# A four-layer decoder on one core: first keys ahead of the statistics, weight splits moved, and cross attention's quantised inputs behind the squares

## The chip, the core and the metric

The kernel is one program on one core of a Trainium2 chip. Its engines are TensorE (PE for its matmuls, PEld for its weight loads), VectorE (DVE), ScalarE (ACT), GpSimd (POOL) and SyncE (SP), which issues the DMAs. The metric is the device time of one execution in microseconds. Three runs of the kernel before took 2043.24 to 2045.09 us, with a median of 2044.54 us.

## What is computed

The reference is a decoder of four layers over x of shape (8, 128, 256), each layer with an attention, a cross attention and a feed-forward part, and each part added to x behind a layer norm. Three parts that follow each other matter here: the experts of layer 1, and the attention and the cross attention of layer 2. Cut to their core:

```python
# layer 1: one shared and seven routed experts (L1f in the kernel)
output = silu(x @ Ws1) * (x @ Wsg) @ Ws2
for e in range(7):
    output = output + _expert_ffn(x, W1[e], Wg[e], W2[e]) * w_e[..., None]
# layer 2, attention (L2a): 16 heads of 16, causal, with a slope per head
attn = softmax(q @ k.T / 4 + alibi + causal); y = attn @ v; out = y @ W_o
# layer 2, cross attention (L2x): 16 query heads, 8 key groups, head size 128
def _div_clamp_fp8(x, scale):
    y = jnp.clip(x.astype(jnp.float32) / scale, -FP8_MAX, FP8_MAX)
    y = y.astype(jnp.bfloat16).astype(jnp.float32)
    return _fp8_roundtrip(y)
q = _ln(linear(_div_clamp_fp8(ln_out, q_in_scale), wq)); k = ...; v = ...
core = _gqa(q, k, v)                 # self part
xout = _gqa(qx, kx, vx)              # part over the context
catq = _div_clamp_fp8(concatenate([core, xout]), proj_smooth)
out = catq @ wproj.T * scales
```

`_div_clamp_fp8` is what the kernel calls quantising: it divides by a scale, clips, and rounds to the grid of an 8-bit float.

## The kernel before, in words

All five engines run hand-ordered instruction lists and meet at counting semaphores. The order on an engine is the order of the Python calls that issue its instructions; nothing is scheduled by a planner. The eight rows of 128 positions of x are called tiles.

**The experts (L1f).** 16 steps s, each one expert on half of the tokens. PE computes the gate and up products (L4025, L4033), ACT the silu (L1808), DVE their product (`L1f_prod`, L2898), PE the down product (L4050), and DVE adds it, weighted, to x (`L1f_add`, L2908, four instructions of 128x256). Beside that, the weights of the next layer are split in three bf16 parts each, high, middle and low: ACT copies the high part (`L2x_hi`, L1833, or `L2q_hi`), a subtraction leaves the rest (`L2x_rest`, L2934 on DVE), ACT copies the middle part (`L2x_mid`, L1838), and a second subtraction gives the low one (`L2x_lo`, L2940 on DVE). p0 to p7 are the pieces of the output projection's weights, q0 to q3 and qx0 to qx3 those of the two query projections. The raw pieces p0 to p7 come by DMA through two buffers, so p7 is loaded (L1034 on SP) only when p6's low part is done.

**The attention (L2a).** One tile per step i. For the first tile PE computes queries and keys (`L2a_qk`, L4107), ACT copies them (`L2a_qTc`, L1904), DVE spreads the keys with a mask (`L2a_keys`, L3030), PE computes the values (`L2a_value`, L4113) and the scores (`L2a_scores`, L4122), DVE adds the bias (`L2a_bias`, L3036) and takes the maximum (L3042), POOL subtracts it (`L2a_sub`, L1320), ACT takes the exponential (L1916), PE transposes (L4130) and multiplies by the values (L4142, L4146), DVE divides (L3046, L3050), and PE projects (L4152). Ahead of it DVE makes the mask (L3057), fills constants (L3058 to L3062) and takes the statistics of tiles 2 to 7 (`L2a_stats`, L3021, L3024), from which ACT computes the factors (L1892, L1894) for POOL's norm (`L2a_norm`, L1316). The splits of p7 and qx0 to qx2 run in these steps, one instruction of ACT and one of POOL in each.

**The cross attention (L2x).** 64 steps i, eight for each tile: four groups of heads in the self part, four in the part over the context. In a step PE projects q, k, v (`L2x_project`, L4223 and L4227 to L4237), ACT squares q and k (L1992, L1994), DVE sums the squares (`L2x_ss`, L3121), ACT computes the factor (L2004, L2008), DVE scales q and k (`L2x_norm`, L3127, L3128), and PE transposes them (`L2x_qkTr`, L4243, L4247), which ends PE's step. The steps overlap: in step i DVE also takes the maximum of the scores of step i-1 (`L2x_max`, L3132), smooths the output of step i-2 (`L2x_smooth`, L3143) and takes step i-1's reciprocal (L3138); ahead of them stands `L2x_magic` for step i-3 (L3149, L3151, L3153), the first half of the quantising of the attention's output, whose second half is POOL's `L2x_cat` (L1356, L1358). POOL also multiplies the probabilities (`L2x_prob`, L1350). In steps i with i % 8 in (4, 5, 6, 7) and i < 56, 28 of the 64, DVE quantises one of the four inputs of the next tile (`L2x_quantise`, L3009, L3013, L3015, L3017), and POOL finishes it (`L2x_quantise_sum`, L1343, L1346).

## Time and profile before

| | |
|---|---|
| median of three runs | 2044.54 us (2043.24 to 2045.09) |
| the profiled execution | 2038.3 us, of which the span is 2036.6 us |
| busy: PE, DVE, ACT, POOL | 1780.2, 1495.5, 1100.1, 1118.3 us (87%, 73%, 54%, 55% of the span) |
| mean granted clock of TensorE | 0.946 |
| first keys of the attention (L3030) | start at 708.35 us |
| first sum of squares of the cross attention (L3121) | starts at 807.50 us |
| last sum of squares of the cross attention | starts at 1291.51 us |

A time in a row is counted from the start of the span. "L12" is line 12 of the kernel before. A row of the timeline gives start, duration, engine, line and operation, and in square brackets how long the engine stood idle before it and what released it. The granted clock is 1.00 at full speed and 0.50 at half.

### The profile page before, as it was taken

Reading aid. Unit: us, or ns where it says so; the run is one execution under the profiler, and the core shown is the slowest. Engines: PE = TensorE matmul, PEld = TensorE weight load, DVE = VectorE, ACT = ScalarE, POOL = GpSimd, SP = SyncE. Lnnn points to the kernel's source line nnn. Section 1 sums busy time; section 2 is a strip of 40 time slices with the busy share of each in tenths; the row PEclk is TensorE's granted clock in tenths of the full one; section 3 lists DMA queues with packets and bytes.
Section 4 is the critical chain, followed back from the end, with each engine's and each line's share of the span. In section 5 each row is a group of like instructions: output and inputs, shape, how many; then the busy total and the mean of one; then the engine's idle time right before and its main releaser. Section 6 shows DMA issues by size and latency. Waiting matters only on the chain.

```text
span 2036.6 us, 30008 instructions
## 1 busy us (share of the span) xinstructions
PE 1780.2 (87%) x10774; PEld 1291.2 (63%) x10822; DVE 1495.5 (73%) x2379; ACT 1100.1 (54%) x2325; POOL 1118.3 (55%) x823
## 2 busy tenths in 40 slices
PE   6777779799999987999999999878888888998998
PEld 5111148555565575777777778767777765667887
DVE  5788952557546675888898888689999877866654
ACT  4444431334423354666666666567677556754443
POOL 4699950212496074555555555599999952223321
PEclk9788889779999998999999999989999979998999
DMA  4211001140110100000000001200000002000000
GB/s 158 61 37 37 0 1 42 39 186 6 67 79 26 42 12 1 1 1 1 1 1 1 1 1 54 74 0 1 1 1 1 27 1 87 1 1 1 6 9 9
DMA packets 21099, 54.89 MB, mean 27 GB/s; under 512 B 8783, under 2 KB 12536, under 8 KB 18648
## 3 DMA queue, kind: packets, MB, share of 16 engines
q1 hardware_dynamic: 20952, 52.97, 7.9%
q8 instruction: 87, 1.43, 0.3%
q14 instruction: 60, 0.49, 0.1%
HBM read 44.57 MB, written 1.05 MB: 22 GB/s over the span
## 4 chain that ended last, share of the span: by engine, by line
PE 57%; DVE 23%; ACT 8%; issue 7%; POOL 4%; DMA 0%; POOLq 0%; DVEq 0%; ACTq 0%
DVE sbuf L2463 3%; PE psum L4388 3%; PE psum L4050 2%; PE psum L4033 2%; PE psum L4223 2%; PE psum L4025 2%; PE psum L3678 2%; PE psum L4286 2%; DVE sbuf L3015 2%; DVE sbuf L3013 2%; PE psum L4255 2%; ACT sbuf L2116 2%; PE psum L4681 1%; PE psum L4235 1%; DVE sbuf L3151 1%
## 5 line engine op out<-in xcount | busy, mean ns | idle before, releaser
L1397 POOL TENSOR_TENSOR sbuf<-sbuf 128x1035 f32<-128x1035 f32 x128 | 245.0, 1943 | 0.9 <-ACT sbuf L2084 0.9
L4388 PE MATMUL psum<-sbuf 128*128 128x128 f32 (+1 forms) x1024 | 146.4, 294 | 56.3 <-ACT sbuf L2116 41.5
L2116 ACT ACTIVATE sbuf<-sbuf 128x1001 f32<-128x1001 f32 (+1 forms) x128 | 142.0, 1142 | 83.0 <-DVE sbuf L3278 58.9
L4388 PEld LDWEIGHTS psum<-sbuf 128*128 128x128 f32 (+1 forms) x1024 | 128.2, 154 | 76.4 <-ACT sbuf L2116 55.1
L1155 POOL TENSOR_TENSOR sbuf<-sbuf 128x1024 f32<-128x1024 f32 x64 | 149.8, 2355 | 16.5 <-DVE sbuf L2463 16.5
L1350 POOL TENSOR_TENSOR sbuf<-sbuf 128x512 f32<-128x512 f32 x64 | 72.8, 1137 | 153.8 <-DVE sbuf L3138 153.8
L2463 DVE TENSOR_TENSOR_SCAN sbuf<-psum,sbuf 128x1024 f32<-128x1024 f32 x64 | 144.6, 2278 | 12.5 <-POOL sbuf L1155 7.6
L3270 DVE SCALAR_TENSOR_TENSOR psum<-sbuf,psum 128x1024 f32<-128x1024 f32 (+1 forms) x96 | 122.3, 1274 | 21.6 <-PE psum L4378 15.1
L3624 PE MATMUL psum<-sbuf 96*128 96x512 bf16 x256 | 81.2, 426 | 60.5 <-DVE sbuf L2463 34.5
L1543 ACT ACTIVATE psum<-psum,sbuf 128x1016 f32<-128x1016 f32 x64 | 68.7, 1081 | 119.0 <-PE psum L3624 119.0
L3278 DVE TENSOR_TENSOR sbuf<-psum,sbuf 128x1024 f32<-128x1024 f32 (+1 forms) x96 | 116.4, 1213 | 3.3
L1356 POOL TENSOR_TENSOR sbuf<-sbuf 128x512 f32<-128x512 bf16 x64 | 77.5, 1212 | 52.7 <-DVE sbuf L3153 51.0
L3624 PEld LDWEIGHTS psum<-sbuf 96*128 96x128 bf16 x256 | 18.4, 101 | 137.1 <-DVE sbuf L2463 67.9
L2024 ACT ACTIVATE sbuf<-psum,sbuf 128x128 f32<-128x128 f32 x256 | 90.4, 365 | 23.5 <-DVE sbuf L3132 21.8
L4223 PE MATMUL psum<-sbuf 128*128 128x512 bf16 x336 | 90.1, 386 | 6.3 <-issue 3.9
L4286 PE MATMUL psum<-sbuf 128*128 128x256 bf16 x768 | 94.3, 273 | 0.9 <-POOL sbuf L1358 0.9
L1471 POOL TENSOR_TENSOR sbuf<-sbuf 128x1024 f32<-128x1024 f32 x16 | 30.7, 1921 | 116.7 <-DVE sbuf L3474 116.6
L3121 DVE TENSOR_REDUCE sbuf<-sbuf 128x6 f32<-128x768 f32 x64 | 60.8, 950 | 40.6 <-ACT sbuf L1994 40.6
L4286 PEld LDWEIGHTS psum<-sbuf 128*128 128x128 bf16 x768 | 74.9, 98 | 17.6 <-POOL sbuf L1358 1.7
L1358 POOL TENSOR_TENSOR sbuf<-sbuf 128x512 bf16<-128x512 f32 x64 | 81.5, 1274 | 5.0
L3657 PE MATMUL psum<-sbuf 128*32 128x512 f32 x256 | 77.7, 738 | 4.3 <-POOL sbuf L1155 4.3
L1405 POOL TENSOR_TENSOR sbuf<-sbuf 128x1024 f32<-128x1024 f32 (+1 forms) x32 | 68.7, 2146 | 19.7 <-DVE sbuf L3270 19.7
(695 smaller groups left out, 4995.3 us busy)
## 6 DMA issues: line engine op xcount, KB each, us to landing
sbuf<-sbuf SPq DMA_DIRECT2D x50, 128.0 KB, 2.4
sbuf<-w_gu_d SPq DMA_DIRECT2D x2, 2048.0 KB, 11.6
sbuf<-w_p_d SPq DMA_DIRECT2D x8, 512.0 KB, 3.7
sbuf<-w_qkv_d SPq DMA_DIRECT2D x3, 768.0 KB, 4.5
sbuf<-w_e_d SPq DMA_DIRECT2D x1, 2048.0 KB, 7.6
sbuf<-w_dn_d SPq DMA_DIRECT2D x1, 2048.0 KB, 18.9
sbuf<-w_q_d SPq DMA_DIRECT2D x1, 2048.0 KB, 7.9
sbuf<-w_qx_d SPq DMA_DIRECT2D x1, 2048.0 KB, 12.4
```

The source lines that it names most:

```text
L1155: pool.tensor_tensor(L0a_hc[i % 4][:, :], L0a_hs[i % 2][:, :], L0a_Cr[g % 4][:, :], ALU.mult).then_inc(hc_done, 1)
L1358: pool.tensor_tensor(cat16[:, :, :], cat[:, :, :], omagic[:, :, :], ALU.subtract).then_inc(cat_done, 1)
L1397: pool.tensor_tensor(P_r[g % 7][:, :, :], rows.unsqueeze(2).to_broadcast([128, 23, 45]), cols.unsqueeze(1).to_broadcast([128, 23, 45]), AL ...
L2024: last = act.activation(prob[:, h, :], L2x_s[:, h, :], ACT.Exp, bias=smax[:, h:h + 1], accum_out=esum[:, h:h + 1])
L2116: act.activation(Q_r[g % 6][:, 0:w], Q_r[g % 6][:, 0:w], ACT.Silu, scale=q8_p[n % 2][:, h:h + 1]).then_inc(silu_done, 1)
L2463: dve.tensor_tensor_scan(L0a_hs[i % 2][:, :], L0a_dAf[i % 2][:, :], L0a_us[i % 3][:, :], 0.0, ALU.mult, ALU.add).then_inc(scan_done, 1)
L3270: dve.scalar_tensor_tensor(M[:, 0:w], Pf_r[g % 7][:, o:o + w], t8_p[n % 2][:, h, 7:8], zps[:, 0:w], ALU.is_ge, ALU.mult).then_inc(mask_don ...
L3278: dve.tensor_tensor(Q_r[g % 6][:, 0:w], Mps[:, 0:w], Pf_r[g % 7][:, o:o + w], ALU.mult).then_inc(prod_done, 1)
L3624: last = pe.matmul(out[:, 512 * h:512 * h + 512], rows, L0a_stack[g % 4][0:96, a, 512 * h:512 * h + 512], start=True, stop=True)
L4223: last = pe.matmul(L2x_q[:, :, :], xs16[n % 2][:, part, c, :], (L2x_q_part, L2x_qx_part)[part](p, g)[:, c, :], start=c == 0 and p == 0, st ...
L4286: last = pe.matmul(L2x_out[:, :], cat16[:, h, :], w_p3[p][:, 4 * (i % 8) + h, :], start=i % 8 == 0 and h == 0 and p == 0, stop=i % 8 == 7 ...
L4388: last = pe.matmul(Gps[0:m, c, :], Q_r[g % 6][:, 128 * c:128 * c + m], ident[:, :], start=h == 0 and c % 4 == 0, stop=h == 7, skip_group_c ...
```

## The change

Nothing is computed in another way; instructions are moved. There are four groups of edits:

1. Ahead of the attention DVE does the first keys before the statistics. The mask and the constants of `L2a_ones` are set in step 12 of the experts.
2. In step 15 of the experts DVE does the low parts of q3 and p5 before the sum of step 14, and no longer the rest of p6.
3. The rest of p6 goes to POOL, whose low part of p6 follows at once; ACT's middle part of p6 goes in front of the attention. So p7, qx0, qx1 and qx2 each go one step earlier in the attention, on ACT and on POOL.
4. In the cross attention DVE quantises the next tile's inputs behind the sum of squares, where it was in front of it.

```diff
-            def L2x_rest_7():
-                pool.wait_ge(hi_done, L2x_start['hi'] + L2_split['p7'])
-                pool.tensor_tensor(p_raw[0][:, :, :], p_raw[0][:, :, :], w_p3[0][:, 28:32, :], ALU.subtract).then_inc(rest_done, 1)
+            def L2x_rest(q):
+                part = slice(4 * q, 4 * q + 4)
+                pool.wait_ge(hi_done, L2x_start['hi'] + L2_split[f'p{q}'])
+                pool.tensor_tensor(p_raw[0][:, :, :], p_raw[0][:, :, :], w_p3[0][:, part, :], ALU.subtract).then_inc(rest_done, 1)
...
+            L2x_rest(6)
+            L2x_lo(6)
             for i in range(8):
...
                 if i == 0:
-                    L2x_lo(6)
+                    L2x_rest(7)
                 if i == 1:
-                    L2x_rest_7()
-                if i == 2:
                     L2x_lo(7)
-                if i in (3, 5, 7):
-                    L2x_qx_rest((i - 3) // 2)
-                if i in (4, 6):
-                    L2x_qx_lo((i - 4) // 2)
+                if i in (2, 4, 6):
+                    L2x_qx_rest((i - 2) // 2)
+                if i in (3, 5):
+                    L2x_qx_lo((i - 3) // 2)
...
                 if s >= 9:
                     L2x_hi(s - 9)
+            L2x_mid(6)
...
                 if i == 0:
-                    L2x_mid(6)
+                    L2x_hi(7)
                 if i == 1:
-                    L2x_hi(7)
-                if i == 2:
                     L2x_mid(7)
...
+                if s == 15:
+                    L2q_lo(3)
+                    L2x_lo(5)
                 if s > 0:
                     L1f_add(s - 1)
...
-                if 9 <= s < 16:
+                if 9 <= s < 15:
                     L2x_rest(s - 9)
+                if s == 12:
+                    dve.tensor_reduce(L2a_mask2[:, :], mask16[:, :].rearrange('p (r h) -> p h r', r=4), AX.X, ALU.add)
+                    dve.memset(L2a_ones[:, 0:16], 1.0)
+                    dve.memset(L2a_ones[:, 16:48], 0.0)
+                    dve.memset(L2a_ones[:, 48:64], 1.0)
...
             dve.memset(L2a_v[1][:, :, 16:48], 0.0).then_inc(const_done, 1)
-            L2a_stats(2, 8)
             dve.wait_ge(const_done, L2a_start['const'] + 1)
             L2a_keys(0)
+            L2a_stats(2, 8)
...
-                if i < 56 and i % 8 in (4, 5, 6, 7):
-                    L2x_quantise(4 * (i // 8 + 1) + i % 8 - 4)
                 if i >= 11 and (i - 3) % 8 == 0:
                     L2x_resid((i - 11) // 8)
                 if i < 64:
                     L2x_ss(i)
+                if i < 56 and i % 8 in (4, 5, 6, 7):
+                    L2x_quantise(4 * (i // 8 + 1) + i % 8 - 4)
```

DVE from the last step of the experts to the first bias of the attention, in the kernel before. L2929, L2940 and L2934 are the low part of q3, the low part of p5 and the rest of p6; L2908 is the sum, L3021 and L3024 the statistics, L3030 the keys, L3036 the bias.

```order
L2929 TENSOR_TENSOR sbuf<-sbuf 128x1024
L2940 TENSOR_TENSOR sbuf<-sbuf 128x1024
L2934 TENSOR_TENSOR sbuf<-sbuf 128x1024
L2908 SCALAR_TENSOR_TENSOR sbuf<-psum,sbuf 128x256 x4
L3057 TENSOR_REDUCE sbuf<-sbuf 128x2
L3058 MEMSET sbuf 128x16
L3059 MEMSET sbuf 128x32
L3060 MEMSET sbuf 128x16
L3061 MEMSET sbuf 128x8x32
L3062 MEMSET sbuf 128x8x32
L3021 BN_STATS sbuf<-sbuf 128x6 x6
L3024 BN_AGGR sbuf<-sbuf 128x2 x6
L3030 TENSOR_TENSOR sbuf<-psum,sbuf 128x512
L3036 TENSOR_TENSOR sbuf<-psum,sbuf 128x1024
```

The same place in the changed kernel, whose line numbers are 0 to 8 higher: L2908 is still the sum, L3038 the keys, L3029 and L3032 the statistics, L3044 the bias.

```order
L2929 TENSOR_TENSOR sbuf<-sbuf 128x1024
L2940 TENSOR_TENSOR sbuf<-sbuf 128x1024
L2908 SCALAR_TENSOR_TENSOR sbuf<-psum,sbuf 128x256 x8
L3065 MEMSET sbuf 128x8x32
L3066 MEMSET sbuf 128x8x32
L3038 TENSOR_TENSOR sbuf<-psum,sbuf 128x512
L3029 BN_STATS sbuf<-sbuf 128x6 x6
L3032 BN_AGGR sbuf<-sbuf 128x2 x6
L3044 TENSOR_TENSOR sbuf<-psum,sbuf 128x1024
```

The rest of p6 and the four small instructions of the mask have left this row, and the keys stand before the statistics.

DVE in one of the 28 steps of the cross attention that quantise an input, in the kernel before, from the reciprocal of one step to the maximum of the next. L3149 to L3153 are `L2x_magic`, L3009 to L3017 `L2x_quantise`, L3121 is the sum of squares and L3132 the maximum.

```order
L3138 RECIPROCAL sbuf<-sbuf 128x4
L3149 TENSOR_SCALAR sbuf<-sbuf 128x512
L3151 TENSOR_SCALAR sbuf<-sbuf 128x512
L3153 TENSOR_SCALAR sbuf<-sbuf 128x512
L3009 TENSOR_TENSOR sbuf<-sbuf 128x256
L3013 TENSOR_SCALAR sbuf<-sbuf 128x256
L3015 TENSOR_SCALAR sbuf<-sbuf 128x256
L3017 TENSOR_SCALAR sbuf<-sbuf 128x256
L3121 TENSOR_REDUCE sbuf<-sbuf 128x6
L3132 TENSOR_REDUCE sbuf<-psum 128x4
```

The same step in the changed kernel, where L3153 to L3157 are `L2x_magic`, L3125 is the sum of squares, L3017 to L3025 are `L2x_quantise` and L3136 is the maximum.

```order
L3142 RECIPROCAL sbuf<-sbuf 128x4
L3153 TENSOR_SCALAR sbuf<-sbuf 128x512
L3155 TENSOR_SCALAR sbuf<-sbuf 128x512
L3157 TENSOR_SCALAR sbuf<-sbuf 128x512
L3125 TENSOR_REDUCE sbuf<-sbuf 128x6
L3017 TENSOR_TENSOR sbuf<-sbuf 128x256
L3021 TENSOR_SCALAR sbuf<-sbuf 128x256
L3023 TENSOR_SCALAR sbuf<-sbuf 128x256
L3025 TENSOR_SCALAR sbuf<-sbuf 128x256
L3136 TENSOR_REDUCE sbuf<-psum 128x4
```

The sum of squares has passed the four instructions of the quantising; the maximum stands behind all five, as it did.

## Rows read from the trace of the kernel before

**Rows 1.** Chain of waits, 690 to 730 us: start, us, what.

```profile
703.63 1.66 DVE sbuf L2908 x4
...
706.12 1.91 DVE sbuf L3021 x6
...
708.43 0.58 DVE sbuf L3030
...
713.05 1.24 DVE sbuf L3036
```

**Rows 2.** Timeline, 696 to 710 us: start, us, engine, line, operation [idle before].

```profile
696.65 1.04 ACT L1833 ACTIVATE sbuf<-sbuf 128x1024 bf16<-128x1024 f32 x1
...
702.69 1.95 PE L4107 MATMUL psum<-sbuf 128*128 128x128 f32 x16
...
704.67 0.38 ACT L1904 ACTIVATE sbuf<-psum 128x256 f32<-128x256 f32 x1 [5.67 <-PE psum L4107]
...
708.80 0.21 ACT L1894 ACTIVATE sbuf<-sbuf 128x6 f32<-128x6 f32 x1
```

**Rows 3.** Stretch 710 to 712 us: busy PE, PEld, DVE, ACT, POOL, granted clock.

```profile
710.00:712.00 2.00, 2.00 (x14) 1.20 (x15) 0.00 (x0) 0.45 (x2) 0.35 (x1) 0.50 0.00 0
```

**Rows 4.** Timeline, 722 to 730 us: load of p7 and what follows.

```profile
722.48 0.33 SPq L1034 DMA_DIRECT2D sbuf<-w_p_d  x1
...
726.15 1.06 ACT L1833 ACTIVATE sbuf<-sbuf 128x1024 bf16<-128x1024 f32 x1 [1.05 <-DMA sbuf<-w_p_d]
...
728.65 0.42 DVE L3050 TENSOR_TENSOR sbuf<-psum,sbuf 128x256 f32<-128x256 f32 x1
...
729.35 1.03 PE L4152 MATMUL psum<-sbuf 128*128 128x256 f32 x4
```

**Rows 5.** DVE timeline of a quantising step of the cross attention.

```profile
901.44 0.68 DVE L3132 TENSOR_REDUCE sbuf<-psum 128x4 f32<-128x512 f32 x1
...
905.29 0.43 DVE L3153 TENSOR_SCALAR sbuf<-sbuf 128x512 f32<-128x512 bf16 x1
...
908.75 0.95 DVE L3121 TENSOR_REDUCE sbuf<-sbuf 128x6 f32<-128x768 f32 x1
909.61 0.68 DVE L3132 TENSOR_REDUCE sbuf<-psum 128x4 f32<-128x512 f32 x1
```

**Rows 6.** ACT timeline of that step: the last square.

```profile
906.28 0.38 ACT L1994 ACTIVATE sbuf<-psum 128x256 f32<-128x256 f32 x1 [0.27 <-PE psum L4229]
```

**Rows 7.** Waits, 860 to 1305 us: total, times, longest.

```profile
PE psum L4243 <- DVE sbuf L3128: 16.9, 25, 0.9
```

**Rows 8.** Timeline of two steps that don't quantise, DVE.

```profile
938.45 0.95 DVE L3121 TENSOR_REDUCE sbuf<-sbuf 128x6 f32<-128x768 f32 x1 [0.83 <-ACT sbuf L1994]
...
945.69 0.95 DVE L3121 TENSOR_REDUCE sbuf<-sbuf 128x6 f32<-128x768 f32 x1 [0.73 <-ACT sbuf L1994]
```

**Rows 9.** Timeline of a step that doesn't quantise: `L2x_magic`'s end, POOL's `L2x_cat`.

```profile
882.73 0.43 DVE L3153 TENSOR_SCALAR sbuf<-sbuf 128x512 f32<-128x512 bf16 x1
...
884.48 1.27 POOL L1358 TENSOR_TENSOR sbuf<-sbuf 128x512 bf16<-128x512 f32 x1
```

**Rows 10.** Timeline, 942 us, DVE and POOL.

```profile
942.75 1.14 POOL L1350 TENSOR_TENSOR sbuf<-sbuf 128x512 f32<-128x512 f32 x1 [2.54 <-DVE sbuf L3138]
...
942.90 1.26 DVE L3149 TENSOR_SCALAR sbuf<-sbuf 128x512 bf16<-128x512 f32 x1
944.20 0.29 DVE L3151 TENSOR_SCALAR sbuf<-sbuf 128x512 uint16<-128x512 uint16 x1
```

**Rows 11.** DVE timeline, a quantising while POOL idles: L3013 to the next L3009.

```profile
791.72 0.29 DVE L3013 TENSOR_SCALAR sbuf<-sbuf 128x256 bf16<-128x256 f32 x1
...
792.51 0.42 DVE L3009 TENSOR_TENSOR sbuf<-sbuf 128x256 f32<-128x256 f32 x1
```

**Rows 12.** A small DVE instruction (ns min/median/max, first and last start) and POOL at 606 us.

```profile
L2874 DVE TENSOR_TENSOR sbuf<-sbuf x2: 188/1798/3409, 535.5 to 606.5; 128x28 f32<-128x28 f32 x2
606.30 7.16 POOL L1248 TENSOR_TENSOR sbuf<-sbuf 128x2048 f32<-128x2048 f32 x2
```

More of the change, by code:

```diff
@@ L1933, in _ @@
                 if i == 0:
-                    L2x_mid(6)
+                    L2x_hi(7)
                 if i == 1:
-                    L2x_hi(7)
-                if i == 2:
                     L2x_mid(7)
+                if i in (2, 4, 6):
+                    L2x_qx_hi((i - 2) // 2)
                 if i in (3, 5, 7):
-                    L2x_qx_hi((i - 3) // 2)
-                if i in (4, 6, 8):
-                    L2x_qx_mid((i - 4) // 2)
+                    L2x_qx_mid((i - 3) // 2)
                 if i < 8:
@@ L2975, in _ @@
                     L1f_next_norm()
-                if 8 <= s < 16:
+                if 8 <= s < 15:
                     if s % 2 == 0:
@@ L2980, in _ @@
                         L2q_lo((s - 8) // 2)
-                if 10 <= s < 16:
+                if 10 <= s < 15:
                     L2x_lo(s - 10)
-                if 9 <= s < 16:
+                if 9 <= s < 15:
                     L2x_rest(s - 9)
+                if s == 12:
[3 more added lines that the diff above has]
+                    dve.memset(L2a_ones[:, 48:64], 1.0)
             def L2x_stats(n):
@@ L3056, in _ @@
             dve.wait_ge(resid_done, L1f_start['resid'] + 64)
-            dve.tensor_reduce(L2a_mask2[:, :], mask16[:, :].rearrange('p (r h) -> p h r', r=4), AX.X, ALU.add)
-            dve.memset(L2a_ones[:, 0:16], 1.0)
-            dve.memset(L2a_ones[:, 16:48], 0.0)
-            dve.memset(L2a_ones[:, 48:64], 1.0)
             dve.memset(L2a_v[0][:, :, 16:48], 0.0)
             dve.memset(L2a_v[1][:, :, 16:48], 0.0).then_inc(const_done, 1)
-            L2a_stats(2, 8)
             dve.wait_ge(const_done, L2a_start['const'] + 1)
             L2a_keys(0)
+            L2a_stats(2, 8)
             dve.wait_ge(factor_done, L2a_start['factor'] + 1)
```

## The prediction, made before the changed kernel was run

> **What bounds the kernel now.** The busy times of the page come first: PE 87% of the span, DVE 73%. Such averages hide the two places that the change touches, so the next view is the chain of waits from the end of the experts to the first bias of the attention. It runs over DVE alone from 703.63 to 709.01 us: the last sum, the small constants, the statistics from 706.12, the first keys from 708.43 (708.35 in the timeline). Then PE computes values and scores, and the first bias starts at 713.05 [rows 1]. But the queries and keys that L3030 needs were copied by ACT at 705.05 (704.67 + 0.38) [rows 2]. So DVE's order, not its input, costs 3.3 us, and PE stands idle so long that its granted clock is 0.50 afterwards, the lower level of 1.2 GHz [rows 3].
>
> The third view is DVE's timeline in a quantising step of the cross attention. From one maximum to the next it takes 909.61 - 901.44 = 8.17 us with no idle time [rows 5], while two sums of squares in steps without quantising are 945.69 - 938.45 = 7.24 apart, and DVE waits there for the squares of ACT [rows 8]. In 25 steps PE waited for DVE's norm [rows 7]. So the quantising steps go at DVE's pace and the others at PE's. The sum of squares starts at 908.75 though its last input was ready at 906.66 [rows 5, 6]: the quantising stands in front of it.
>
> **First keys ahead of the statistics (edits 1 and 2).** PE leaves the last down product at 702.69, where `L2a_qk` starts; that time stays, since the sum of step 14, which `L2a_qk` waits for, moves behind two splits but still ends some 2 us before it. The last two of the four sums (1.66 us for four) [rows 1] then end near 703.7, and the two constants that are left are part of the 0.83 us between 705.29 and 706.12 [rows 1]: DVE is ready by 704.5. The keys start when ACT's copy ends, at 705.1, not 708.35: 3.25 us earlier. The statistics take 2.31 us (706.12 to 708.43) and now lie beside PE's values and scores, from 705.75 to 708.1.
>
> What is late next? Values and scores took 713.05 - 709.01 = 4.04 us at half clock [rows 1, 3]. At full clock I estimate 2.3 from them (half, and some fixed part). PE now idles 1.2 us (704.64 to 705.8) where it idled 4.4. If the clock stays up, the scores end at 708.1, with the statistics, and the first bias starts at 708.2 instead of 713.05: 4.85 earlier. If it falls all the same, it is 705.75 + 4.04 = 709.8: 3.25 earlier. I take 4.85, as the gap is about a quarter of the old one. ACT's factors move behind the statistics, to 708.7 (they ended 0.6 behind them, at 709.01 [rows 2]), and its copy of the values queues behind them; that is ahead of the 709.3 which the next tile's `L2a_qk` needs to be as early as the first bias demands, as its copy is due only after two biases and a maximum of DVE. The mask's four small instructions go into step 12, where DVE waits for PE in each step: nothing. Without that cover they would cost some 0.3 us.
>
> **The weight splits (edits 2 and 3).** ACT's high part of p6 ends at 697.69 [rows 2]. POOL, idle there, does the rest of p6 in about 2 us (half of one of L1248's two took 1.8 [rows 12]), ACT the middle part in 1.06 [rows 4], POOL the low part in 2: 703 us, or 704 if the rest must let DVE's low part of p5 go first. ACT's new wait stands in front of its table load and its copy of the first queries, and what is queued behind it is due at 704.67, after an idle time of 5.67 us [rows 2]: middle part and table load end by 703.3, so 1.4 us are left. Should POOL's rest go first and hold DVE's split by 2 us, the sum of step 14 ends at 702.6, just in time for PE's 702.69. So: nothing, bounded by a few tenths. On SP's queue nothing but the load of p7 changes its time. It is issued at 703 to 704 instead of 722.48, and ACT does not wait for it: before, ACT stood 1.05 us for that DMA at 726.15, and the transposes behind it held PE so that the projection (L4152) started at 729.35 although its input was ready at 729.07 [rows 4]. That returns 0.25 us (0.28 at most), since DVE's division is late next. All later splits keep the same slot one step earlier, with the same distance to what they wait for: nothing. At the end of the attention ACT and POOL each have one instruction less, where they idle.
>
> Attention in all: -4.85 - 0.25 = -5.1 us (-3.5 at half clock).
>
> **Quantising behind the squares (edit 4), 28 steps.** I count from the start of L3153, the last instruction of `L2x_magic`, to the next maximum. Before: 909.61 - 905.29 = 4.32 us [rows 5]. After, the sum of squares starts when its input is ready, at +1.37 (906.66), and takes 0.86 (908.75 to 909.61) [rows 5, 6]: it ends at +2.25. Meanwhile POOL does the two instructions of `L2x_cat`, which end at 884.48 + 1.27 - 882.73 = +3.02 [rows 9]. L3009, first of the quantising, is now issued in the middle of them. It has two inputs in SBUF. Does POOL hold such an instruction? L2874, also with two inputs in SBUF, took 0.19 us once and 3.41 us the other time, when it started under POOL's two long instructions of 606.30 [rows 12]: yes, to POOL's end. How fast it comes out of it is shown by L3149, as long as L3009 when free: POOL's L1350 ended at 942.75 + 1.14 = 943.89, and DVE's next instruction started at 944.20, 0.31 later [rows 10]. After L3009 POOL is idle until the quantising is done, and the other three take 792.51 - 791.72 = 0.79 us [rows 11]. The maximum then starts at 3.02 + 0.31 + 0.79 = +4.12, not +4.32. The rest of the loop, maximum, norm, smoothing, reciprocal, `L2x_magic`, is unchanged and still DVE's. Gain: 0.20 per step, 28 x 0.20 = 5.6 us. The bounds: 0.93 per step (26 us), where the step falls to PE's 7.24; and a loss of 0.5, below.
>
> Two pages of the Trainium skill differ on this. "Advanced Engine Details and Errata" (VectorE Performance Modes) names only two-port instructions as those that GpSimd blocks, and "VectorE: DVE Perf Modes" (Why `tensor_tensor` can't do 2×_2P or 4×) says that a tensor_tensor can't run in such a mode; by these two L3009 would run free, which is the second case below. "SBUF — State Buffer" (SBUF: two separate sides) adds instructions with two SBUF inputs, against a GpSimd instruction that reads SBUF; by that the sum is the one above, and the 3.41 us of L2874 agree with it.
>
> **Sum.** -5.1 - 5.6 = -10.7 us. The profiled execution took 2038.3 us; the change would make it 2027.6. The median of the runs is 6.2 us above the profiled one, and I carry the difference over: 2044.54 - 10.7 = 2033.8 us. All that follows the cross attention is ordered by semaphores and moves with it.
>
> **The rivals.** A change of 0.2%, 4.1 us, is about what can be told from none here: faster means below 2040.4, slower above 2048.6.
>
> A. As forecast, 2033.8, between 2031 and 2037: 52%.
>
> B. POOL does not hold L3009. It then runs at +2.25 under POOL's second instruction, only L3013 waits for its end, and at most 0.5 us of the quantising is left behind 3.02 + 0.31: the maximum at +3.8 or earlier, 0.5 to 0.93 per step. With 0.6: 28 x 0.6 = 16.8, and with the attention's 5.1 the time is 2022.6. For it speaks only that L3009 has never yet been issued under a POOL instruction in this loop, so no row shows it held; against it stands L2874. 15%.
>
> C. The cross attention gains nothing, because the held instructions come out of POOL's shadow 0.2 us later than L3149 did; the attention alone gives 5.1, so 2039.4, or 3.5 with PE still at half clock there, so 2041.0. For it speaks how small 0.2 is beside waits of a microsecond. 22%: 13% at full clock, 9% at half.
>
> D. Slower: the sum of squares slips in front of POOL's second `L2x_cat` instruction instead of under it. Then L3009 takes its turn before POOL (0.46), POOL's instruction (1.27) follows and holds L3013, and the maximum comes at 2.25 + 0.46 + 1.27 + 0.31 + 0.5 = +4.8, 0.45 later than before: 28 x 0.45 = 12.6, less the attention's 5.1: 2052. It decides from where POOL's second instruction, now at 884.48 - 882.73 = +1.75 [rows 9], starts after the sum's end at +2.25, half a microsecond later than the row. That POOL has been on time in its steps speaks against it. 8%.
>
> Left: both gains are lost in PE's clock elsewhere, within 0.2%: 3%.
>
> Faster: 52 + 15 + 13 = 80%, same 9 + 3 = 12%, slower 8%. The range from 2020 to 2042 holds A, C and nearly all of B.
>
> **What would show it.** Right: the first keys near 705.1 and the first bias near 708.2 us; granted clock 1.00 from 706 to 710; no wait of ACT for the p7 DMA; L3009's successor in the 28 steps some 0.3 us behind POOL's `L2x_cat`, L3009 lasting 1 us or more, the later three unhindered; steps of 7.97 us; first to last sum of squares 484.0 - 5.6 = 478.4 us. Wrong: L3009 at 0.42 us in those steps and steps near 7.5 (B); steps of 8.17 (C); L3013 at over 1 us and steps above 8.2 (D); the copy of the first queries on ACT later than 704.7, which would break the cover of the p6 split.

## The result and the profile after

The changed kernel takes 2029.61 us, the median of 4 runs (2022.84 to 2032.61), the kernel before 2044.82 beside it (4 runs, 2043.24 to 2045.86). The ratio is 0.9921, with a 95% interval of 0.9906 to 0.9937: 16.2 us less, 12.9 to 19.2. The forecast of 2033.8 lies 4.2 us above the median, and the forecast gain of 10.7 us lies outside that interval. The profiled execution took 2031.22 us (span 2029.5).

The spans of the two profiles differ by 7.1 us only. Before its first `L2a_qk`, where the edits save nothing, the profiled run of before was 8.5 us quicker (702.69 us against 711.18; a second profile of before has 711.38). So I count all positions from the start of the first `L2a_qk` on PE. Positions read so, in us:

```
kernel           first keys  first bias  second sum of sq.  last sum of sq.
before               5.66      10.36        112.93             588.82
before, again        5.66      10.61        110.68             586.51
changed              2.47       5.56        103.94             573.37
```

**The attention's start.** First the end of the experts on DVE and POOL, then what PE, ACT and DVE do up to the first bias, in the timeline of the changed kernel (start, us, engine, line, operation, idle before); they answer to [rows 1, 2]. Rows between those shown are left out.

```profile
706.27 1.22 DVE L2940 TENSOR_TENSOR sbuf<-sbuf 128x1024 bf16<-128x1024 f32 x1
706.27 3.21 POOL L1293 TENSOR_TENSOR sbuf<-sbuf 128x1024 f32<-128x1024 f32 x1 [48.98 <-ACT sbuf L1834]
709.51 1.06 ACT L1839 ACTIVATE sbuf<-sbuf 128x1024 bf16<-128x1024 f32 x1 [3.32 <-POOL sbuf L1293]
710.59 1.28 ACT L1926 ACT_TABLE_LOAD   x1
711.18 1.95 PE L4111 MATMUL psum<-sbuf 128*128 128x128 f32 x16
713.17 0.38 ACT L1906 ACTIVATE sbuf<-psum 128x256 f32<-128x256 f32 x1 [1.29 <-PE psum L4111]
713.65 0.69 DVE L3038 TENSOR_TENSOR sbuf<-psum,sbuf 128x512 f32<-128x512 f32 x1 [0.73 <-ACT sbuf L1906]
714.26 2.05 DVE L3029 BATCH_NORM_STATS2 sbuf<-sbuf 128x6 f32<-128x256 f32 x6
714.40 1.13 PE L4117 MATMUL psum<-sbuf 128*128 128x256 f32 x4 [1.27 <-DVE sbuf L3038]
716.74 1.22 DVE L3044 TENSOR_TENSOR sbuf<-psum,sbuf 128x1024 f32<-128x1024 f32 x1
```

DVE now waits 0.73 us for ACT's copy (L1906), the first keys follow it, and the statistics lie beside values and scores. ACT had its extra work (L1839, table load) done by 711.87, 1.3 us before the copy was due. POOL's rest of p6 (L1293), issued with DVE's L2940, took 3.21 us and not 2, and ACT's middle part waited for it; the DVE instruction took its usual 1.22. The granted clock stays at its upper level, 2.4 GHz, where [rows 3] had 0.50 (window, busy PE, PEld, DVE, ACT, POOL, clock, DMA share, GB/s):

```profile
714.00:716.00 2.00, 1.60 (x13) 1.20 (x17) 2.00 (x7) 0.00 (x0) 0.00 (x0) 1.00 0.69 240
```

**The load of p7.** ACT no longer waits for its DMA, and PE's projection waits for DVE's division, as [rows 4] would have it without that wait: it starts 16.08 us behind the first bias, where it was 16.30. In the second profile of before it was 17.01, because ACT's wait was 1.75 us there and not 1.05:

```profile
735.79 1.06 ACT L1833 ACTIVATE sbuf<-sbuf 128x1024 bf16<-128x1024 f32 x1 [1.75 <-DMA sbuf<-w_p_d]
```

In all five profiles with the old order of the splits (before twice, experiments 3 and 5) the projection starts 15.25 to 15.26 us plus that wait behind the first bias. The wait was 1.05 to 1.75 us, so its end is worth 0.2 to 0.9 us. The changed kernel:

```profile
732.35 0.42 DVE L3058 TENSOR_TENSOR sbuf<-psum,sbuf 128x256 f32<-128x256 f32 x1
732.82 1.13 PE L4156 MATMUL psum<-sbuf 128*128 128x256 f32 x4 [0.41 <-DVE sbuf L3058]
```

**A quantising step**, DVE and POOL, to be laid beside [rows 5, 6, 9, 10]:

```profile
903.75 0.43 DVE L3157 TENSOR_SCALAR sbuf<-sbuf 128x512 f32<-128x512 bf16 x1
904.65 0.38 ACT L1994 ACTIVATE sbuf<-psum 128x256 f32<-128x256 f32 x1 [0.27 <-PE psum L4233]
905.06 0.95 DVE L3125 TENSOR_REDUCE sbuf<-sbuf 128x6 f32<-128x768 f32 x1 [0.88 <-ACT sbuf L1994]
905.50 1.27 POOL L1359 TENSOR_TENSOR sbuf<-sbuf 128x512 bf16<-128x512 f32 x1
905.93 1.12 DVE L3017 TENSOR_TENSOR sbuf<-sbuf 128x256 f32<-128x256 f32 x1
907.09 0.29 DVE L3021 TENSOR_SCALAR sbuf<-sbuf 128x256 bf16<-128x256 f32 x1
...
907.89 0.68 DVE L3136 TENSOR_REDUCE sbuf<-psum 128x4 f32<-128x512 f32 x1
...
909.55 0.66 PE L4247 MATMUL psum<-sbuf 128*128 128x128 f32 x4 [0.52 <-DVE sbuf L3132]
...
915.87 0.68 DVE L3136 TENSOR_REDUCE sbuf<-psum 128x4 f32<-128x512 f32 x1
```

From L3157 to the maximum it takes 4.14 us (before 4.32), from one maximum to the next 7.98 (before 8.17). L3017 runs under POOL's L1359 and lasts 1.12 us instead of 0.42: it is held, which in this text means that an instruction lasts longer than when free and ends with or just behind the other engine's. L3021 starts 0.32 us behind POOL's end. All 32 quantisings (ns min/median/max, first and last start):

```profile
L3017 DVE TENSOR_TENSOR sbuf<-sbuf x32: 415/1120/1132, 793.7 to 1226.5; 128x256 f32<-128x256 f32 x32
```

PE's waits for the norm from 850 to 1250 us (total, times, longest), first before, then changed; [rows 7] counts from 860 to 1305:

```profile
PE psum L4243 <- DVE sbuf L3128: 17.7, 26, 0.9
PE psum L4247 <- DVE sbuf L3132: 11.7, 26, 0.5
```

### The profile page after: what moved, and what is told of

It is laid out like the page before. It is cut to its first block, busy times and chain, and to the rows that moved or that the text cites. A ratio compares the mean times of both kernels' runs of the same rounds, so it can differ in the third digit from the quotient of the medians.

```text
span 2029.5 us, 30008 instructions
## 1 busy us (share of the span) xinstructions
PE 1784.7 (88%) x10774; PEld 1293.0 (64%) x10822; DVE 1459.2 (72%) x2378; ACT 1097.0 (54%) x2325; POOL 1118.3 (55%) x824
## 3 DMA queue, kind: packets, MB, share of 16 engines
HBM read 44.57 MB, written 1.05 MB: 22 GB/s over the span
## 4 chain that ended last, share of the span: by engine, by line
PE 63%; DVE 17%; ACT 8%; issue 7%; POOL 5%; DMA 0%; POOLq 0%; DVEq 0%; ACTq 0%
PE psum L4227 4%; DVE sbuf L2463 4%; PE psum L4392 3%; PE psum L4029 3%; PE psum L4037 3%; PE psum L4054 3%; PE psum L4290 2%; PE psum L3682 2%; POOL sbuf L1398 2%; PE psum L4247 2%; PE psum L4259 2%; PE psum L4275 2%; PE psum L4685 1%; DVE sbuf L3017 1%; ACT sbuf L2116 1%
## 5 line engine op out<-in xcount | busy, mean ns | idle before, releaser
L3125 DVE TENSOR_REDUCE sbuf<-sbuf 128x6 f32<-128x768 f32 x64 | 61.0, 953 | 65.2 <-ACT sbuf L1994 65.2
L1357 POOL TENSOR_TENSOR sbuf<-sbuf 128x512 f32<-128x512 bf16 x64 | 74.3, 1161 | 52.3 <-DVE sbuf L3157 50.6
L1359 POOL TENSOR_TENSOR sbuf<-sbuf 128x512 bf16<-128x512 f32 x64 | 81.5, 1274 | 5.0
```

Of the source, the lines that this page charges most:

```text
L1359: pool.tensor_tensor(cat16[:, :, :], cat[:, :, :], omagic[:, :, :], ALU.subtract).then_inc(cat_done, 1)
```

## The experiments

Times of the kernel before beside them: 2043.58 us with the first four, 2045.18 with experiments 5 to 8, 2045.69 with experiment 9 and with the second profiles of experiments 5 and 6.

**1. The kernel before once more.** No edit.

> The kernel before, unchanged: a second trace of it. Theory: the stretches at half clock around 708 to 714 us (cost 1.6 us) come back, since the idle time of PE in front of them is part of the order; those at 787 to 816 us, which cost the kernel before some 4 us against the changed one, come from an idle time of PE that both kernels have, so their length may differ between two executions of one kernel by 2 us and more. Rival: they are a property of the kernel, and the distance from the first bias of the attention (L3036) to the second sum of squares of the cross attention (L3121) is 102.57 us again, to 0.3 us.

2044.92 us. The half-clock stretch after PE's idle gap recurs: first bias at 10.61. Positions that nothing explains but the clock move: from the first bias to the second sum of squares it takes 100.07 us, in the first profile 102.57. From there to the last sum of squares the two agree: 475.83 and 475.89. A pair of profiles tells 1 us in the cross attention, but not at the end of the attention. The second profile is 2.5 us shorter there although its wait for p7's DMA is 0.7 us longer. The rival, that the 102.57 us are a property of the kernel, falls.

**2. The changed kernel without edit 4.**

```diff
+                if i < 56 and i % 8 in (4, 5, 6, 7):
+                    L2x_quantise(4 * (i // 8 + 1) + i % 8 - 4)
                 if i >= 11 and (i - 3) % 8 == 0:
                     L2x_resid((i - 11) // 8)
                 if i < 64:
                     L2x_ss(i)
-                if i < 56 and i % 8 in (4, 5, 6, 7):
-                    L2x_quantise(4 * (i // 8 + 1) + i % 8 - 4)
```

> The changed kernel with the quantising back in front of the sum of squares: edits 1 to 3 alone. Theory: first bias 5.6 us behind the start of the first query matmul (10.36 before), the p7 load 0.2 us, quantising steps of 8.17 us as before; 5 us faster than before, 2039.5. What is above that can only come from the clock around 787 to 816 us (up to 4 us, to 2035.5). Rival: the quantising's move gave most of the 15 us and this kernel is within 2 us of the one before.

2033.61 us, ratio 0.9955 (0.994 to 0.997): 9.2 us less than before, 6.1 to 12.3. First bias at 5.56 as in the changed kernel, second to last sum of squares 475.47 us, as in before. So the attention's part is larger than the 5.1 forecast, and what is more lies between the first bias and the second sum of squares: 98.32 us here and 98.38 in the changed kernel, against 102.57 and 100.07. The time is 2 us below the lowest that I had expected (2035.5).

**3. Edit 4 alone, on the kernel before.** The same condition and its call moved the other way.

> The kernel before with the quantising behind the sum of squares and nothing else: edit 4 alone. Theory: quantising steps of 7.98 us, 28 x 0.20 = 5.6 us faster, 2039; first bias 10.36 us behind the first query matmul, as before. Rival: edit 4 also shortens the stretches at half clock at the start of the cross attention, and the kernel is 9 us or more faster, 2036 or less.

2038.29 us, ratio 0.9975 (0.9965 to 0.9985): 5.1 us less, 3.1 to 7.2. Second to last sum of squares 469.82 us, 6.0 less than before. With 9.2 from experiment 2 that makes 14.3 of the 16.2 us, within the intervals. The rival, 9 us or more, falls.

**4. The quantising behind the norm.**

```diff
                 if i < 64:
                     L2x_ss(i)
-                if i < 56 and i % 8 in (4, 5, 6, 7):
-                    L2x_quantise(4 * (i // 8 + 1) + i % 8 - 4)
                 if 1 <= i < 65:
                     L2x_max(i - 1)
                 if i < 64:
                     L2x_norm(i)
+                if i < 56 and i % 8 in (4, 5, 6, 7):
+                    L2x_quantise(4 * (i // 8 + 1) + i % 8 - 4)
```

> The changed kernel with the quantising one place further back, behind the norm (sum of squares, maximum, norm, quantising, smoothing). Theory: L3009's counterpart is now issued when POOL has finished its cat, takes 0.42 us and no longer 1.12, and neither maximum nor norm waits for the quantising: the steps fall from 7.98 us to PE's pace of 7.24 to 7.5, 28 x 0.5 to 0.74 = 14 to 20 us, 2010 to 2016. Rival: the quantising now delays smoothing, reciprocal and the magic of the step by 1.25 us, and with them POOL's cat and its probabilities, which the next transposes and projections wait for: the steps stay at 7.9 us or more, 2028 to 2032; if the delay goes on to PE in full, 8.5 us and 2044.

2017.37 us (4 runs, 2015.97 to 2023.12), ratio 0.988 (0.986 to 0.99): 24.5 us less than before, faster than both kernels, though not the 2010 to 2016 us expected. DVE and POOL in its quantising steps:

```profile
904.41 1.26 POOL L1359 TENSOR_TENSOR sbuf<-sbuf 128x512 bf16<-128x512 f32 x1
904.49 0.69 DVE L3136 TENSOR_REDUCE sbuf<-psum 128x4 f32<-128x512 f32 x1 [0.54 <-PE psum L4259]
905.69 0.41 DVE L3132 TENSOR_TENSOR sbuf<-psum,sbuf 128x256 f32<-128x256 f32 x1
906.02 0.41 DVE L3017 TENSOR_TENSOR sbuf<-sbuf 128x256 f32<-128x256 f32 x1
...
908.96 1.09 POOL L1351 TENSOR_TENSOR sbuf<-sbuf 128x512 f32<-128x512 f32 x1
909.18 1.15 DVE L3157 TENSOR_SCALAR sbuf<-sbuf 128x512 f32<-128x512 bf16 x1
...
912.26 0.69 DVE L3136 TENSOR_REDUCE sbuf<-psum 128x4 f32<-128x512 f32 x1 [0.82 <-PE psum L4259]
```

The maximum now waits for PE's scores, L3017 is free of POOL (0.41), and the steps take 7.24 and 7.77 us by turns. From 855 to 1290 us PE has no wait for the norm among its longest; the longest is for POOL, 5.2 us in all:

```profile
PE psum L4290 <- POOL sbuf L1359: 5.2, 14, 0.6
```

**5. Edit 1's order of keys and statistics alone, on the kernel before**, profiled twice.

```diff
-            L2a_stats(2, 8)
             dve.wait_ge(const_done, L2a_start['const'] + 1)
             L2a_keys(0)
+            L2a_stats(2, 8)
```

> The kernel before with edit 1 alone: the first keys stand in front of the statistics of the six tiles; the mask, the constants and the weight splits stay where they were. DVE is then free for the keys at about 706.1 us of before's trace (3.4 us after the start of the first L2a_qk, where it was 5.66), no longer bound by ACT's copy. PE's gap is about 2.2 us. If the clock stays up, values and scores take 3.1 us from the keys, as in the changed kernel: first bias 6.5 us after L2a_qk, 3.9 us sooner than before, total about 4 us under before. If the gap is long enough for the clock to fall, they take 4.7: first bias at 8.1, 2.2 us sooner. Theory one (the gain at the first bias comes from the order of keys and statistics, and the mask move adds only about 1 us): this, and the end of the attention (last residual) also up to 1.6 us sooner if the half-clock stretch there depends on where the extra instructions of ACT and POOL lie, or unchanged if edit 3 is its cause. Rival: the gain comes mostly from edits 2 and 3 (splits taken off DVE's last sums); then the first bias moves by under 1.5 us.

> The kernel with edit 1 alone, a second look. Its first profile had PE idle for 2.26 us before the first values and a granted clock of 0.50 afterwards, so that the first bias came 8.13 us after the first L2a_qk. If the clock's fall belongs to what the kernel does there, it recurs at the same place; if it is chance of one execution, values and scores are at full clock and the first bias comes at 6.5.

2042.28 us, ratio 0.9981 (0.9967 to 0.9996): 3.9 us less, 0.8 to 6.7 (the execution of the second profile took 2034.88 us). The keys start at 3.47 and 3.46. PE idles 2.26 us in both, but goes on at half clock in the first (first bias at 8.13) and at full clock in the second (6.56). The first profile:

```profile
717.33 1.76 PE L4113 MATMUL psum<-sbuf 128*128 128x256 f32 x4 [2.26 <-DVE sbuf L3030]
719.02 2.09 PE L4122 MATMUL psum<-sbuf 32*128 32x256 f32 x16
```

and the second:

```profile
706.90 1.13 PE L4113 MATMUL psum<-sbuf 128*128 128x256 f32 x4 [2.26 <-DVE sbuf L3030]
707.96 1.15 PE L4122 MATMUL psum<-sbuf 32*128 32x256 f32 x16
```

The rival falls: the order of keys and statistics alone brings 2.2 or 3.8 us of the 4.8 at the first bias against the first profile of before (2.5 or 4.05 of the 5.05 against the second), as the clock falls or not. The end of the attention gains nothing from it: 102.83 and 102.98 us from first bias to second sum of squares.

**6. The changed kernel with the statistics in front of the keys again**, also profiled twice. The same lines moved back.

> The changed kernel with the statistics of the six tiles back in front of the first keys, all else as changed. DVE starts the statistics about 1.6 us after the first L2a_qk and ends them at 3.9, so the keys start at 3.9 and not at 2.47. With PE's clock up the first bias comes at 7.0 us after L2a_qk, 1.4 later than in the changed kernel; with the clock down after a gap of 2.5 us at 8.6, 3 later. The total is 1.4 to 3 us above the changed kernel. If the end of the attention keeps the changed kernel's time (84.3 us from first bias to last residual), the shorter end is due to edits 2 and 3 and not to the order of the keys; if it goes back to 86.0, the order of the keys sets it.

> The changed kernel with the statistics in front of the first keys, a second look. Its first profile had PE idle for 2.93 us, longer than the 2.26 us of the kernel with edit 1 alone, and yet a granted clock of 1.00 afterwards (first bias at 7.22). If the length of the gap alone decided, that was chance and this time the clock is at 0.50 and the first bias at 8.7; if it recurs at full clock, the length of the gap alone is not what decides.

2034.08 us, ratio 0.9937 (0.992 to 0.9955), so some 3 us above the changed kernel by the ratios (the execution of the second profile took 2030.7 us). The keys start at 4.16, PE idles 2.93 us and goes on at full clock both times; first bias at 7.22:

```profile
709.53 1.13 PE L4117 MATMUL psum<-sbuf 128*128 128x256 f32 x4 [2.93 <-DVE sbuf L3038]
```

So an idle time of 2.26 us was followed by half clock in one execution and by full clock in another, 2.93 us by full clock twice, 4.4 us by half clock in three profiles (before twice, experiment 3). The length of the gap alone doesn't decide, but the counts go with it: after 1.27 us the clock stayed up in all six profiles that have this gap, after 2.26 or 2.93 in three of four, after 4.4 in none of three.

The end of the attention goes back to 102.44 and 102.47 us. That doesn't show that the order of the keys shortens it. These two profiles reach the first `L2a_qk` at 704.66 and 705.79 us, the changed kernel's at 711.18; and all four profiles that reach it before 706 us (these two, the first of before, the second of experiment 5) have 102.4 to 103.0. The nine that reach it later have 98.3 to 102.8. So what the execution did earlier is a rival that no run separates from the edits. What differs is PE's clock. Windows of 4 us, first of the changed kernel:

```profile
786.00:790.00 4.00, 2.33 (x67) 2.06 (x68) 3.97 (x5) 2.05 (x3) 2.92 (x2) 1.00 0.01 4
...
798.00:802.00 4.00, 1.13 (x4) 0.68 (x4) 2.71 (x5) 0.00 (x0) 1.16 (x2) 0.89 0.00 0
802.00:806.00 4.00, 1.15 (x3) 0.59 (x5) 1.79 (x7) 0.00 (x0) 2.06 (x3) 0.50 0.02 4
806.00:810.00 4.00, 3.34 (x11) 2.15 (x9) 0.95 (x1) 1.38 (x4) 2.92 (x3) 0.76 0.00 0
```

then of this experiment, whose work lies 4.9 us earlier:

```profile
786.00:790.00 4.00, 3.48 (x13) 3.02 (x14) 0.90 (x4) 2.65 (x4) 0.09 (x1) 0.57 0.00 0
...
798.00:802.00 4.00, 0.37 (x1) 0.28 (x3) 2.39 (x9) 0.00 (x0) 1.51 (x2) 0.50 0.00 0
802.00:806.00 4.00, 4.00 (x11) 2.54 (x10) 0.14 (x1) 0.89 (x2) 3.47 (x3) 0.50 0.00 0
```

The changed kernel spends one stretch at half clock, around the gap in front of the cross attention; this one has two before its first sum of squares. The same operation, the projection of the attention (line, mean ns, idle), from 786 to 818 us, in the kernel before:

```profile
L4152 PE MATMUL psum<-sbuf 128*128 128x256 f32 x8 | 3.7, 613 | 3.4 <-DVE sbuf L3050 3.4
```

and in the changed kernel:

```profile
L4156 PE MATMUL psum<-sbuf 128*128 128x256 f32 x8 | 2.3, 405 | 3.6 <-DVE sbuf L3058 3.6
```

**7. The quantising behind the maximum**, between the changed kernel's place and that of experiment 4.

```diff
                 if i < 64:
                     L2x_ss(i)
-                if i < 56 and i % 8 in (4, 5, 6, 7):
-                    L2x_quantise(4 * (i // 8 + 1) + i % 8 - 4)
                 if 1 <= i < 65:
                     L2x_max(i - 1)
+                if i < 56 and i % 8 in (4, 5, 6, 7):
+                    L2x_quantise(4 * (i // 8 + 1) + i % 8 - 4)
```

> The changed kernel with the quantising of the next tile behind the maximum instead of in front of it. POOL's two instructions are over by then, so L3017 lasts 0.41 us, not 1.12. But the norm that PE's transposes wait for comes 1.25 us later than where the quantising stands behind it; PE had about 1.0 us of slack there. Theory (both count: the hold by POOL and what the quantising stands in front of): steps of 7.5 to 7.8 us, total 2017 to 2025, between the changed kernel and the one with the quantising behind the norm. Rival one (only the hold counts): the same as behind the norm, 2017. Rival two (only the place in front of maximum and norm counts, and the hold was never worth anything): near the changed kernel, 2028 or more.

2037.26 us, ratio 0.996 (0.9945 to 0.9975), so the theory and rival one fall. Of rival two only the number, 2028 or more, holds, not its reason: L3017 is free of POOL, and yet the steps take 8.19 us, as long as before. From the second to the last sum of squares it takes 477.82 us, 1.9 more than before. DVE and PE:

```profile
908.08 0.69 DVE L3136 TENSOR_REDUCE sbuf<-psum 128x4 f32<-128x512 f32 x1 [0.83 <-PE psum L4259]
908.69 0.41 DVE L3017 TENSOR_TENSOR sbuf<-sbuf 128x256 f32<-128x256 f32 x1
...
910.54 0.41 DVE L3132 TENSOR_TENSOR sbuf<-psum,sbuf 128x256 f32<-128x256 f32 x1
911.00 0.66 PE L4247 MATMUL psum<-sbuf 128*128 128x128 f32 x4 [0.73 <-DVE sbuf L3132]
```

The maximum waits for PE, so what stands between it and the norm lies on the loop from scores over maximum and norm to PE's next transposes. From the maximum's start to the norm's end it takes 2.87 us (908.08 to 910.95), from there to the next maximum 5.32, together 8.19. In experiment 4 the first part is 1.61 us (904.49 to 906.10), so that this loop needs 6.93 us, and the slack under PE's 7.24 was 0.3 us; I had taken 1.0, from a step where PE was late by its own wait of 0.36 us for POOL.

Seen from PE, the lengths of the steps add up in one way: 7.24 us, PE's wait, and some 0.2 us more. With waits for the norm of 0.52 and 0.73 that gives 7.96 and 8.17 (measured 7.98 and 8.19), with before's 0.71 8.15 (8.17), with experiment 4's 0.36 for POOL 7.8 (7.77). This sum doesn't say what makes PE wait. In the changed kernel that is the loop of DVE and POOL: 3.84 us from the maximum to L3157, 4.14 from there over POOL's L1359 and L3017 to the next maximum.

**8. L3017 with one input.** The division by the input scales is left out, a constant stands in its place.

```diff
-                dve.tensor_tensor(xs, unT0[:, :, :], inrc[:, v, :].unsqueeze(2).to_broadcast([128, 2, 128]), ALU.mult).then_inc(ratio_done, 1)
+                dve.tensor_scalar(xs, unT0[:, :, :], 0.5, 1.0, ALU.mult, ALU.mult).then_inc(ratio_done, 1)
```

> The changed kernel with L3017, a multiplication of two SBUF operands, replaced by a multiplication of the same data by a constant (one SBUF input; the division by the input scales is left out), at the same place under POOL's second L2x_cat instruction. Theory (POOL holds L3017 because it has two inputs in SBUF): the instruction lasts 0.3 us and starts at once, 2.3 us after L3157's predecessor; if the three behind it are free as well, the maximum starts 0.6 to 0.75 us sooner per step, steps of 7.24 to 7.5 us, total 2010 to 2017. Rival one: any DVE instruction of this size but a reduction is held: 1 us again, steps of 7.9, total 2029. Rival two: L3017 is free but the next, L3021 with its 16 bit output, is held in its place: also 2029, with L3021 at 0.7 us or more.

2029.03 us, ratio 0.991 (0.9889 to 0.9932). What the first rival says holds for this instruction: it needs 0.28 us when free, and still takes 0.99 under POOL.

```profile
908.32 1.27 POOL L1359 TENSOR_TENSOR sbuf<-sbuf 128x512 bf16<-128x512 f32 x1
908.75 0.99 DVE L3017 TENSOR_SCALAR sbuf<-sbuf 128x256 f32<-128x256 f32 x1
909.77 0.29 DVE L3021 TENSOR_SCALAR sbuf<-sbuf 128x256 bf16<-128x256 f32 x1
```

It ends 0.15 us behind POOL; L3017 with two inputs ended 0.28 behind. Hence steps of 7.85 us, 0.13 less. Two inputs in SBUF are one way to be held, not the only one.

**9. POOL's sums behind the next `L2x_cat`**, on top of experiment 4.

```diff
                 if i >= 3:
                     L2x_cat(i - 3)
-                if i < 56 and i % 8 in (4, 5, 6, 7):
-                    L2x_quantise_sum(4 * (i // 8 + 1) + i % 8 - 4)
+                if i < 56 and i % 8 in (5, 6, 7):
+                    L2x_quantise_sum(4 * (i // 8 + 1) + i % 8 - 5)
+                if i < 56 and i % 8 == 7:
+                    L2x_quantise_sum(4 * (i // 8 + 1) + 3)
                 if 1 <= i < 65:
                     L2x_prob(i - 1)
```

> The kernel with the quantising behind the norm (2017.37 us), and in addition POOL's two sums of the quantising (L1344, L1347) moved from the end of their step to behind L2x_cat of the next one, where POOL idles; the last of each four keeps its step. Theory: what was left over PE's 7.24 us there is DVE's L3157, held 0.7 us by POOL's L1351 because that one started late behind the sums; the projection (L4290) then waits 0.36 us for POOL. With the sums gone L1351 starts 0.9 us sooner, L3157 lasts 0.43 us, L2x_cat comes 0.4 us sooner, and three of four quantising steps fall from 7.51 to 7.24-7.30 us: 21 x 0.24 = 5 us less, about 2012. Rival: the sums in their new place hold DVE's maximum or norm, or the last sum comes too late for PE; then the steps are 7.5 or more and the total 2017 or above.

2023.28 us (5 runs, 2017.37 to 2024.48), ratio 0.9885 (0.9865 to 0.9905): no gain over experiment 4, and not the 2012 us expected. L3159 (L3157 there) is free, as expected, but now the sum holds the quantising's first instruction, here L3019:

```profile
904.78 0.43 DVE L3159 TENSOR_SCALAR sbuf<-sbuf 128x512 f32<-128x512 bf16 x1
...
908.51 0.73 POOL L1347 TENSOR_TENSOR sbuf<-sbuf 128x256 bf16<-128x256 f32 x1
908.54 0.98 DVE L3019 TENSOR_TENSOR sbuf<-sbuf 128x256 f32<-128x256 f32 x1
```

The hold has moved, and second to last sum of squares takes 464.61 us against 458.80 in experiment 4.

## Why the prediction was right, point by point

**What bounds the kernel.** Right. The loop's limit is PE at 7.24 us a step, as [rows 8] had it; in experiment 4, where DVE's norm doesn't keep PE waiting, the quantising steps take 7.51 us on average. In the changed kernel they still go at the pace of DVE and POOL, as forecast.

**First keys ahead of the statistics: -4.85 us.** Measured -4.80 against the first profile of before, -5.05 against the second (its first bias is at 10.61). The keys start 3.2 us sooner, bound by ACT's copy; values and scores take 3.09 us from the keys' start at full clock. The clock was a choice there and it came out right, and the gap, 1.27 us, was near the 1.2 forecast. The reason given, that the gap is a quarter of the old one, is neither refuted nor proved: all six profiles with that gap kept the clock, but experiments 5 and 6 show that length alone doesn't settle it, and that 2.26 us wasn't safe.

**The weight splits: nothing, and -0.25 us for p7.** -0.22 measured at the first projection against the first profile of before, -0.93 against the second. The bound of 0.28 was too small: it took the 1.05 us wait for the DMA of one profile as fixed, and the profiles with the old order have 1.05 to 1.75. The rest of p6 took 3.21 us on POOL, and nothing on the path waited for it: ACT had 1.3 us left, 1.4 was forecast.

**Not in the sum: the end of the attention.** I let everything from the first bias to the cross attention shift as a block, but for the p7 wait. It became 4.2 us shorter than in the first profile of before, 1.7 than in the second, of which p7 explains 0.2 and 0.9. In the first pair the rest goes with granted clock, as the windows of experiment 6 show it; the 0.8 left in the second pair is argued, not shown. This is the term that was mis-sized: -0.25 should have been -1.7 to -4.2. That something more is gained than the forecast 5.1 us doesn't hang on the profiles: experiment 2, which has the attention's edits alone, gained 9.2 us (6.1 to 12.3) in its timed runs. By how much the edits move the clock stays open. Six profiles of kernels with the changed keys and splits have 98.3 to 98.4 us in five and 99.8 in one; those without one or both (seven) have 100.1 to 103.0, and four of these seven are the ones that reach `L2a_qk` before 706 us.

**Quantising behind the squares: 28 x 0.20 = 5.6 us.** Steps of 7.98 us, 7.97 forecast; L3157 to maximum +4.14, +4.12 forecast; 6.4 to 6.5 us from second to last sum of squares in the profiles, 6.0 in experiment 3's, 5.1 (3.1 to 7.2) in its timed runs. Over the forecast lie the step behind each group of four, 6.93 us from maximum to maximum instead of 7.03, which the sum left out, and one step of before that took 8.53 us and not 8.18. First to last sum of squares came to 475.5 us, not 478.4: 2.0 of the difference is the first step, 6.12 us instead of 8.12, a matter of clock again. Rival B falls with L3017's 1.12 us. The Trainium skill, "SBUF — State Buffer" (SBUF: two separate sides), has the rule for two SBUF inputs that the prediction cited, and L3017 agrees with it. Experiment 8's instruction has one such input and is held too, 0.99 us. The Trainium skill, "GPSIMD Engine Reference" (1. Specifications), names contention with DVE instructions in a two-port mode beside those with two SBUF inputs. Whether experiment 8's instruction ran in such a mode no run here shows; that it takes 0.28 us when free, against 0.42 with two inputs, would fit.

**The rivals.** C falls, since the held instruction is followed 0.32 us behind POOL's end, as after L3149. D falls: POOL's second instruction starts at +1.75 in the changed kernel too (905.50 - 903.75), 0.4 us ahead of the sum of squares' end. D's price has a slip: 2.25 + 0.46 + 1.27 + 0.31 + 0.5 - 4.32 is 0.47, not 0.45, which would make it 2052.6 and change nothing. The median of 2029.61 lies below A's own 2031 to 2037, though the mechanism was A's, and above B's 2022.6, whose mechanism is refuted. That it fell into the range from 2020 to 2042 owes something to luck: 5.5 us of gain came from what the sum hadn't in it, and the only case given to the clock elsewhere (3%) had it as a loss.

**The total.** -10.7 forecast, -16.2 measured (12.9 to 19.2). In the profiles, from the first `L2a_qk` to the last sum of squares, it is -15.4 against the first profile of before and -13.1 against the second: -4.8 or -5.05 at the first bias, -4.2 or -1.7 at the end of the attention, -6.5 or -6.4 in the cross attention. The second profile stands for the usual run better: its execution took 2044.92 us, where the median is 2044.82, while the first took 2038.3, and only 3 of the 43 runs of before that stand beside the experiments took less. How often before is at 102.6 and how often at 100.1 stays open all the same, as does what sets the clock there.

## What to carry to other kernels

When work leaves the path of one engine, look at which loop it lies on afterwards, and not only at whether it still waits: 1.25 us of quantising cost 0.95 a step between maximum and norm, 0.74 in front of the maximum, where POOL held it, and 0.27 on average behind the norm, by way of POOL. Before a DVE instruction over SBUF data is put beside a POOL instruction, count it as ending with POOL's, whether it has one input or two, unless a trace shows its kind free, as the sum of squares below; filling POOL's idle time elsewhere may only move the hold. And where PE idles as long as the 2.26 us here, price the stretch behind at both clocks and take several profiles.

## What the runs showed of the hardware that was not expected

- The hold works both ways. POOL's L1293 and DVE's L2940 started together at 706.27 us; DVE took its 1.22 us and POOL 3.21, where the same L1293 took 2.14 at 724.01. All eight profiles with edit 3 have 3.21 or 3.22 there.
- A held instruction ended 0.15 us (experiment 8) to 0.28 us behind POOL's, and DVE's next one started 0.18 to 0.32 us behind it, although the held ones take 0.28 and 0.42 us when free.
- A sum of squares (L3125, one input, a reduction) isn't held: it took 0.94 to 0.95 us in all 64 steps of experiment 7, though in the quantising steps it starts under one POOL instruction (L1357, 905.40 to 906.56) and ends under the next (it ran from 906.30 to 907.25).
- PE's wait costs more than its length: some 0.2 us a step on top of 7.24 and the wait, in steps of 7.98, 8.17 and 8.19 us. Why is not shown.
- The kernel's span varies by where PE's clock falls, in stages that no edit touches: 702.69 or 711.38 us to the first `L2a_qk` of the same kernel, 741 to 745 us behind the last sum of squares.
